# Macaron block (FFN, attention, FFN) on one core: weighted values of a step ahead of the next step's scores instead of between them

## What is computed

```
x = x + 0.5 * ffn(layernorm(x))
x = x + attention(layernorm(x))
x = x + 0.5 * ffn(layernorm(x))
```

```
att = einsum('bhqd,bhkd->bhqk', q, k) / sqrt(16)
att = where(k > q, -1e9, att)
att = softmax(att, axis=-1)
out = einsum('bhqk,bhkd->bhqd', att, v)
return einsum('bsd,od->bso', out, w_out)
```

## Time and profile before

| | us |
|---|---|
| median of 3 runs | 1109.41 |
| span of the profiled execution | 1107.3 |
| TensorE matmul busy in it | 1029.0 (93%) |
| VectorE busy | 714.0 (64%) |
| ScalarE busy | 447.6 (40%) |
| GpSimd busy | 119.3 (11%) |
| attention's steps, first exponential to the end | 381.65 to 844.6 |

### The profile page before, as it was taken

One profiled execution on the slowest core, in us unless ns is written; L12 is line 12 of the kernel. 1 busy time (PEld: TensorE's weight loads), 2 busy tenths in 40 slices (PEclk: granted clock), 3 DMA queues, 4 the chain that ended last, 5 costly groups with the idle time before them and its releaser, 6 DMA issues.

```text
span 1107.3 us, 16107 instructions
## 1 busy us (share of the span) xinstructions
PE 1029.0 (93%) x6208; PEld 473.7 (43%) x6208; DVE 714.0 (64%) x1128; ACT 447.6 (40%) x859; POOL 119.3 (11%) x147
## 2 busy tenths in 40 slices
PE   1779999999999599999999999999999999999998
PEld 1335545454555344333333333333324454544544
DVE  4786273654645588888887898887802836546362
ACT  1324020211214256555567666677786212112020
POOL 3665410000133000100000000000000100001000
PEclk9988999999999799999999999999999999999999
DMA  7000000000019600200020000000000000000000
GB/s 234 0 1 1 1 1 1 0 0 1 1 38 141 136 11 2 30 2 1 1 31 2 1 1 2 1 2 1 1 1 1 1 1 20 1 19 0 20 1 20
DMA packets 21964, 20.19 MB, mean 18 GB/s; under 512 B 4232, under 2 KB 21640, under 8 KB 21896
## 3 DMA queue, kind: packets, MB, share of 16 engines
q1 hardware_dynamic: 19784, 17.17, 7.5%
q10 hardware_dynamic: 2112, 2.10, 0.6%
HBM read 12.78 MB, written 6.29 MB: 17 GB/s over the span
## 4 chain that ended last, share of the span: by engine, by line
PE 82%; DVE 9%; issue 2%; POOL 2%; DMA 2%; ACT 1%; SPq 0%; DVEq 0%; ACTq 0%; POOLq 0%
PE ps L1037 12%; PE ps L940 10%; PE ps L1001 10%; PE ps L1023 10%; PE ps L908 10%; PE ps L909 10%; PE ps L910 10%; PE ps L941 5%; DVE m_part L820 4%; PE ps L1010 2%; DMA qk_split<-wreg 2%; PE ps L902 1%; PE ps L893 1%; PE ps L969 1%; DVE oT L626 1%
## 5 line engine op out<-in xcount | busy, mean ns | idle before, releaser
L563 ACT ACTIVATE wreg<-ps 128x512 f32<-128x512 f32 (+3 forms) x640 | 304.1, 536 | 152.9 <-PE ps L1023 78.0
L820 DVE TENSOR_REDUCE m_part<-ps 128x1 f32<-128x1024 f32 (+7 forms) x320 | 326.6, 1060 | 58.2 <-PE ps L1010 29.9
L519 ACT ACTIVATE wreg<-ps,gelu_in 128x512 f32<-128x512 f32 x128 | 88.0, 687 | 351.5 <-PE ps L910 351.5
L1023 PE MATMUL ps<-qreg,kreg 128*128 128x512 f16 (+3 forms) x640 | 181.0, 351 | 10.4 <-DMA qreg<-m_rows 8.7
L691 DVE SCALAR_TENSOR_TENSOR wreg<-ps,kappa,wreg 128x512 f32<-128x512 f32 x128 | 96.0, 750 | 145.6 <-PE ps L910 145.5
L1001 PE MATMUL ps<-kreg,qreg 128*128 128x512 f16 (+3 forms) x640 | 175.3, 351 | 7.7 <-DVE m_part L820 5.6
L940 PE MATMUL ps<-wd,qreg 128*128 128x512 f16 x512 | 166.8, 379 | 0.0
L1037 PE MATMUL ps<-wreg,v 128*17 128x512 f32 (+3 forms) x1280 | 149.8, 534 | 0.8 <-ACT oT L493 0.8
L941 PE MATMUL ps<-wd,qreg 128*128 128x256 f16 x512 | 139.6, 273 | 0.0
L1023 PEld LDWEIGHTS ps<-qreg,kreg 128*128 128x128 f16 x640 | 58.9, 97 | 131.1 <-ACT wreg L563 91.4
L908 PE MATMUL ps<-xT,wg 128*128 128x512 f16 x256 | 98.8, 386 | 3.1 <-DVE xT L671 2.4
(11 more groups left out here) (126 smaller groups left out, 931.4 us busy)
## 6 DMA issues: line engine op xcount, KB each, us to landing
qk_split<-wreg SPq DMA_DIRECT2D x4, 1024.0 KB, 9.1
kreg<-qk_split SPq DMA_DIRECT2D x24, 128.0 KB, 4.1
qreg<-qk_split SPq DMA_DIRECT2D x24, 128.0 KB, 7.8
xres<-in_L_attn_x ACTq DMA_DIRECT2D x4, 512.0 KB, 7.6
out_x<-xres SPq DMA_DIRECT2D x4, 512.0 KB, 2.9
kreg<-in_L_ffn_gate_W_packed SPq DMA_DIRECT2D x1, 1024.0 KB, 6.8
kreg<-in_L_ffn_up_W_packed SPq DMA_DIRECT2D x1, 1024.0 KB, 9.3
kreg<-in_L_ffn_down_W_packed SPq DMA_DIRECT2D x1, 1024.0 KB, 10.2
```

The lines of the kernel that those rows point to most:

```text
L519: act.activation(gelu_ring[:, n % 3, :], bank(n % 2), ACT.Gelu_apprx_tanh, scale=gelu_in[:, 0:1]).then_inc(s_gelu, 1)
L563: act.activation(wreg[:, b % 8, 0:CT - q0], bank(score_bank[b], CT - q0), ACT.Exp, scale=EXP_SCALE).then_inc(s_p, 1)
L820: dve.tensor_reduce(m_part[:, r, part, col:col + 8 * (cnt - 1) + 1:8], src, AX.X, ALU.max)\
L1023: last = pe.matmul(dst, kreg[:, pair, P * j:P * j + P], qreg[:, c % 2, h % 2, pair, q0:CT], start=True, stop=not diag)
```

## The change

One number: the weighted values of the step before become the first piece of the list instead of the third. The order on TensorE was: scores 0 and 1, score 2, weighted values of t-1, score 3. It becomes: weighted values of t-1, scores 0 and 1, score 2, score 3. The shares of planned items keep their formula, so with two items the first now stands behind score 1 (before: behind score 2), the second behind score 3 as before. Nothing else changes; no instruction is added or removed.

```
@@ -1077,7 +1077,7 @@
                 parts = [lambda: (scores(t, 0), scores(t, 1)), lambda: scores(t, 2), lambda: scores(t, 3)]
                 if t:
-                    parts.insert(2, lambda: weighted_values(t - 1))
+                    parts.insert(0, lambda: weighted_values(t - 1))
                 for k, part in enumerate(parts):
                     part()
                     for u in plan[t][len(plan[t]) * k // len(parts):len(plan[t]) * (k + 1) // len(parts)]:
                         planned(*u)
```

## The result

The changed kernel takes 1200.49 us (median of 4 runs, 1199.5 to 1201.51), the kernel before 1109.78 us beside it. The ratio is 1.082, with a 95% interval of 1.0805 to 1.0835. The forecast was 1188 us with a range of 1166 to 1210: the direction, the place and most of the size came out; 12 us were missed, and most of them turn out to belong to a cost of their own.

The account below looks back on a forecast made before the run. TensorE bounds most attention steps and ScalarE the last sixteen; the change closes a chain between them. Chain passes of 509 us plus 33 for heavy steps give 542 against 463, +79 on 1109.4: 1188 us, range 1166 to 1210.

Parts of the forecast that it names:

- the chain: Attention steps: TensorE and ScalarE take turns, exponential 3, block, score 0, four exponentials; 509 us over all passes.
- full light step: Step of 512 queries outside the heavy steps: 0.05 + 0.96 + 0.42 + 2.07 = 3.50 us, against 2.82 before.
- pass 15: Last attention pass, with no units beside it: 52.8 us for 32.04, +20.7.
- One sign: Weighted values' loads (L1037) in the changed trace: the last pair, head 3, comes well after the first six.
- The copy out of bank 3: First step of each pass: the copy behind the fourth exponential joins the chain, 0.5 us a pass.
- the diagonal steps: Four steps of each pass, with narrowing queries: 3.57, 3.07, 2.41 and 1.85 us, together 10.9.
- the heavy steps: 28 steps paced by VectorE's slots: the chain fits under their present times; 33 us added above the chain.
- The prediction's own sign: Full steps in the changed trace: if they differ with the number of items, the chain does not set them.
- the fourth rival: Heavy steps: VectorE's slot waits and the chain add up, at most 0.7 us each, +20, 1208 us; chance 0.12.
- Cover: Item behind score 3 hides ScalarE's latency, so only steps without units pay: +23.5, 1133 us; chance 0.06.
- The shorter step: Load of head 3: exponential 3 is done by the block's turn, so full steps shorten; -4 us, 1105; chance 0.03.
- The third rival: TensorE's clock falls to 1.2 GHz: 1203 us if in pass 15 alone, beside units too 1250; chance 0.05.

Follow-up runs that it names:

- Experiments 1: The run lag2: the change, but with weighted values of two steps before at the head of the step; 1127.76 us.
- 4: Every unit computes and reduces only its last 128 keys: in the changed kernel 1168.05 us, in the kernel before 1037.56 us.
- 5: The changed kernel with one more 0.5 us ScalarE copy in every step, behind the exponentials; 1198.47 us.
- Experiment 2: The kernel before with the weighted values behind all four scores (pos3, 1115.23 us) or behind scores 0 and 1 (pos1, 1141.86 us).
- lag2: The change, but the weighted values at the head of the step are those of two steps before; 1127.76 us, ratio 1.0148 to the kernel before.
- pos3: The kernel before with the weighted values of the step before moved behind all four scores; 1115.23 us, ratio 1.0037.
- experiment 3: The changed kernel with all planned items of a step behind score 3; 1249.5 us in one run.
- 8: The kernel before with the weighted values behind all four scores in pass 15 only; 1107.53 us, ratio 0.9987.
- pos1: The kernel before with the weighted values of the step before moved behind scores 0 and 1; 1141.86 us, ratio 1.0277.

## Why the prediction was right, and where 12 us were missing

**The bound and the chain: right.** A full light step was forecast at 3.50 and measured at 3.51; pass 15 at +20.7 and measured at +20.0. Every link was on a row: 0.06 (0.05 forecast) and 0.96 are in the timeline above, the burst is 2.06 (2.07 forecast). Experiments 1, 4 and 5 show it from three sides: remove the wait and 73 us go; remove the work and the light steps stay; add to ScalarE and nothing moves. Experiment 2 shows that the same sum predicts another place (2.52, measured 2.53).

One sign came out otherwise: the last pair of loads was to come well after the first six, but all four pairs come 0.49 us apart, each behind its own exponential. The chain runs through the last pair alone, so the sum did not depend on it.

**The copy out of bank 3 and the diagonal steps: right, term by term.** In pass 15, from the end of one step's last exponential to the next, the first step took 2.87 us (2.89 forecast), the second 4.02 (3.50 and 0.5 for the copy), the diagonal ones 3.57, 3.09, 2.39 and 1.70 (3.57, 3.07, 2.41, 1.85). Passes 13 and 14 together went from 85.9 to 107.1 us, +21.2 for a forecast of +19.7; most of what is over lies in their steps with three items (3.75 and 3.83). With the units' work taken away pass 14 took 52.88 us, for 52.8 forecast.

**What failed: that everything but the chain stays as it was.** Two sentences carried it: TensorE's own work "fits inside when there are up to three units", and in the heavy steps "the chain fits under what they take already". Both treat the planned items as a load; their place relative to the block was a part of the change that I named in the front part and priced at nothing. In a light full step with three units it costs 0.1 to 0.4 us above the chain (most of them took 3.62 to 3.93). The prediction's own sign applies there: where steps differ with the number of items, the chain is not what sets them. In the heavy steps the four stretches of the earlier trace rows were forecast unchanged at 62.4 us and took 65.2.

This accounts for most of the 12 us. Above the 509 us of the chain the prediction put 33; the windows hold 553.4 us, so it was 44. By the spacing of the first exponentials, 25 steps with three items that stood below the chain in the kernel before now stand 7.4 us above it together, where the forecast had nothing; the four stretches hold 2.8 more.

Now the heavy steps. One of their steps in the changed kernel:

```profile
733.66 0.44 PE L973 MATMUL ps<-ident,att 128*128 128x128 f32 x2
...
734.58 0.66 PE L969 MATMUL ps<-ident,oT 128*128 128x128 f32 x4 [0.47 <-DVE xres L796]
...
735.16 1.05 PE L1037 MATMUL ps<-wreg,v 128*17 128x512 f32 x8
735.27 0.26 DVE L783 RECIPROCAL recip<-ps 128x16 f32<-128x16 f32 x1
735.56 0.42 DVE L784 TENSOR_TENSOR att<-ps,recip 128x256 f32<-128x256 f32 x1
...
736.15 0.61 PE L1001 MATMUL ps<-kreg,qreg 128*128 128x512 f16 x2
...
736.79 1.23 DVE L820 TENSOR_REDUCE m_part<-ps 128x1 f32<-128x1024 f32 x1 [0.80 <-PE ps L1001]
```

VectorE, the bound here, runs dry for 0.80 us: behind the last item only two short instructions (0.26 and 0.42) are queued for it, the block takes TensorE for a microsecond, and the next unit comes after that. In the same step before, the block started behind two units that gave VectorE 2.36 us of work:

```profile
688.02 2.36 DVE L820 TENSOR_REDUCE m_part<-ps 128x1 f32<-128x1024 f32 x2
...
688.56 1.05 PE L1037 MATMUL ps<-wreg,v 128*17 128x512 f32 x8
```

The argument against the fourth rival, that VectorE "has up to two slots queued, 2.4 us", took the largest items for the typical ones. So the fourth rival was partly true, and not only in heavy steps. The total stayed within the range by the margins that the prediction had given to its terms.

**How the 90 us divide,** by the medians of runs that differ in one thing: the wait, 73 (the change against lag2); the place of the items around the block, 12.5 (lag2 against pos3); the remaining 4 (pos3 against the kernel before) were not taken apart further. The kernel before was 1.4 us slower beside lag2 and pos3 than beside the change, so the wait may be 1 or 2 us more. The shares also depend on the order in which the costs are taken away: a step with three items of pass 14 takes 3.83 us in the change and in lag2 alike, because the wait for the slot and the chain overlap there.

**The other rivals.** Cover is refuted by experiment 3. The shorter step never appeared in the change, but its decision point was sound: where head 3 is not waited for, pass 15 gains 0.13 us a step (experiments 2 and 8). The clock stayed at 1.00 in pass 15. The third rival's picture, 1.8 us of matmuls in a step of 3.5, was off as well: with the heads starting one behind the other some matmul was in flight for 49.58 of 52.06 us. So what the Trainium skill, "TensorE: Matmul & The Clock Gate", section "A second HAM failure mode: psum-queue depth-cycling", tells of short idles between groups was hardly put to the test here.

## What to carry to other kernels

When two engines hand work to each other inside a loop, add up the latencies around the ring, not the work: moving the consumer directly behind the last producer made a ring of 3.51 us out of a step with 2.82 us of work, and no engine's rate, no cover and no removal of other work changed it. Before moving a long block, also ask what it stood between: here it was the pause that let a third engine empty its buffers, and that second cost was a sixth of the first. Delaying a consumer by one more step only helps if the ring of buffers on the other side is read early enough; check both rings, and whether they close only together.

## What the runs showed of the hardware that was not expected

Matmuls on different columns of the array need not start together to overlap. Each head's pair of loads starts as soon as its own exponential is there: in the step above the pairs came 0.49 us apart, and three matmuls in a row of some 0.6 us each, the two of head 0 and the first of head 1, lie within 1.09 us (898.01 to 899.10), so head 1 started while head 0 was still in flight. From the last head's load to the next score's load there were 0.96 us in the change and 0.97 in pos1, whether the heads before it came 0.49 us apart or together, against 0.98 for the whole block with all heads ready.

Back-to-back exponentials are 0.48 to 0.49 us apart (1.91 us for four in pass 15 of pos3) even in the pass where they looked like 0.51. The longer figure, 2.04 for four, went with the block ahead of score 3; with the block behind it the step is 1.91 us.
